# Final stage of a layer norm and mixture-of-experts kernel: the sum of shared and picked rows moves from VectorE to TensorE, and the normalising reads PSUM

## The chip, the core and the metric

The kernel runs on one core of a Trainium2 chip. The metric is the device time of one execution in microseconds (us), the median of several. Work is spread over TensorE (matmuls), VectorE, ScalarE, GpSimd and the DMA queues that SyncE and GpSimd issue to.

## The reference

The input x is 4 sequences of 1024 tokens with 128 features, 4096 tokens in all. Two sublayers follow each other, each closed by a layer norm without gain:

```python
x = layernorm(x + memory_mixer(x))            # cumulative sums of weighted cos/sin features, queries, silu, W_out
logits = x @ router_w.T                       # 8 experts, the best two are taken
out = sum_e mlp_e(x) * combine[:, e] + shared_mlp(x)   # mlp: square(relu(x @ w_fc.T)) @ w_proj.T, 512 wide
x = layernorm(x + out)                        # mean and variance over the 128 features, eps 1e-5
```

The last line is what this case is about. For one token it needs x plus the shared MLP (the "shared row"), the two expert results that the token was sent for (the "picked rows", each already multiplied by its weight), their sum, its mean and variance, and (sum - mean) / sqrt(variance + eps).

## The kernel before

Five functions make the program, and each hands every engine its piece in turn: memory (the mixer), dispatch (first layer norm, router, shared MLP, tokens written to a table by expert), routed (the expert MLPs) and finish. The first two take about 339 us of the span. routed goes over 46 tiles, 25 of 256 rows and then 21 of 128. For each tile SyncE loads rows of the table, TensorE transposes them (L1376), multiplies by the up weights into the tensors ph (L1388), ScalarE applies relu and square (L1434, L1443), TensorE multiplies by the down weights into po (L1401), VectorE scales by the router's weight (L1485) and GpSimd scatters the rows to pick_scratch in HBM, two places for each token. The four tensors ph, unused, po and px of routed take PSUM banks 0 to 6 (ph has two buffers of two banks), one bank is free.

dispatch leaves in y_all, in SBUF, x plus the shared MLP for all 4096 tokens: 32 columns of 128 tokens, 128 features each (L1193).

finish works in 8 groups of four columns, 512 tokens, 128 partitions by 512 numbers. Group g has a PSUM bank of its own, both[g].

- SyncE waits for the last scatters (L1527), then issues 16 loads (L1531), two for each group, 256 KB each, and after them 8 stores (L1537), each behind the ScalarE work of its group.
- TensorE (L1550) waits for the two loads of a group and adds the two picked rows by two matmuls with the identity into both[g]. Float32 matmuls stand in the trace as two passes each, so a group shows as four.
- VectorE adds the shared rows (add, L1578: both[g] + y_all into res, in SBUF), takes statistics (measure, L1586 bn_stats and L1590 bn_aggr, four of each), and in invert the reciprocal of the root (L1596) and the shift, -mean times it (L1598).
- ScalarE takes the square root of variance plus eps (L1561) and normalises, one instruction for each 128 by 128 column, scale and shift from SBUF (L1566).

The order on VectorE and ScalarE is written out by hand:

```python
            add(0)
            measure(0)
            for g in range(NG):
                if g + 1 < NG:
                    add(g + 1)
                invert(g)
                if g + 1 < NG:
                    measure(g + 1)
```

ScalarE takes the groups in turn, root and then four normalising instructions. Buffers res, stats, mv, xo and so on have S = 4 copies, so from group 4 on there are waits for the stores of earlier groups.

Of the kernel before, what the change touches and what calls it, by code (L numbers as in the profile page):

```python
# [14 lines left out]
P = 128  # L15
# [14 lines left out]
GT = 4  # L30
# [29 lines left out]
RoutedStage = namedtuple("RoutedStage", "sync scalar gpsimd tensor vector scattered")  # L60
# [1221 lines left out]
def routed(nc, outer, dis, ident, w1, w2, expert, start, table, pick_dram):  # L1282
# [4 lines left out]
    with ExitStack() as c:  # L1287
# [172 lines left out]
        def vector(dve):  # L1460
# [17 lines left out]
            def body(t, u):  # L1478
# [5 lines left out]
                for h in range(height(t)):  # L1484
# [6 lines left out]
                           scattered=[(scattered[t % U], passes(t)) for t in range(TILES - U, TILES)])  # L1491


def finish(nc, outer, rou, ident, y_all, eps, warm, pick_dram, out):

    with ExitStack() as c:
# [6 lines left out]
        S = 4  # L1503
        pick = sb("pick", [P, 2, NT, D])
        res = sb("res", [P, S, GT, D])
        stats = sb("stats", [P, S, GT, 6])
        mv = sb("mv", [P, S, GT, 2])
        std = sb("std", [P, S, GT])
        rstd = sb("rstd", [P, S, GT])
        shift = sb("shift", [P, S, GT])  # L1510
        xo = sb("xo", [P, S, GT, D])
# [3 lines left out]
        res_done = sem("res_done")  # L1515
# [5 lines left out]
        xo_done = sem("xo_done")  # L1521
        eps_set = sem("eps_set")
        stored = [sem(f"stored{i}") for i in range(S)]

        def sync(sp):
# [9 lines left out]
            def store(g):  # L1535
                sp.wait_ge(xo_done, g + 1)
                sp.dma_start(out[:, g * P:(g + 1) * P, :].rearrange("b p d -> p b d"), xo[:, g % S]  # L1537
                             ).then_inc(stored[g % S], 16)
# [4 lines left out]
            for i in range(S):  # L1543
                sp.wait_ge(stored[i], 16 * NG // S)

        def tensor(pe):
            for g in range(NG):
                pe.wait_ge(picked[g], 32)
                for r in range(2):
                    last = nc.tensor.matmul(both[g][:], ident[:],  # L1550
                                            pick[:, r, g * GT:(g + 1) * GT, :].rearrange("p t d -> p (t d)"),
                                            start=(r == 0), stop=(r == 1))
                last.then_inc(both_done, 1)

        def scalar(act):
            act.wait_ge(eps_set, 1)
            nc.scalar.activation(warm[:], eps[:], ACT.Sqrt)
            for g in range(NG):
                s = g % S
                act.wait_ge(var_done, g + 1)  # L1560
                nc.scalar.activation(std[:, s], mv[:, s, :, 1], ACT.Sqrt, bias=eps[:]).then_inc(std_done, 1)  # L1561
                act.wait_ge(shift_done, g + 1)
                if g >= S:
                    act.wait_ge(stored[s], 16 * (g // S))
                for t in range(GT):
                    last = nc.scalar.activation(xo[:, s, t, :], res[:, s, t, :], ACT.Identity,  # L1566
                                                bias=shift[:, s, t:t + 1], scale=rstd[:, s, t:t + 1])
                last.then_inc(xo_done, 1)

        def vector(dve):  # L1570
            nc.vector.memset(eps[:], EPS).then_inc(eps_set, 1)

            def add(g):
                s = g % S
                dve.wait_ge(both_done, g + 1)
                if g >= S:
                    dve.wait_ge(xo_done, g - S + 1)
                nc.vector.tensor_tensor(res[:, s].rearrange("p t d -> p (t d)"), both[g][:],  # L1578
                                        y_all[:, g * GT:(g + 1) * GT, :].rearrange("p t d -> p (t d)"), ALU.add
                                        ).then_inc(res_done, 1)  # L1580

            def measure(g):
                s = g % S
                dve.wait_ge(res_done, g + 1)
                for t in range(GT):
                    last = nc.vector.bn_stats(stats[:, s, t, :], res[:, s, t, :])  # L1586
                last.then_inc(stats_done, 1)
                dve.wait_ge(stats_done, g + 1)
                for t in range(GT):
                    last = nc.vector.bn_aggr(mv[:, s, t, :], stats[:, s, t, :])  # L1590
                last.then_inc(var_done, 1)

            def invert(g):
                s = g % S
                dve.wait_ge(std_done, g + 1)
                nc.vector.reciprocal(rstd[:, s], std[:, s]).then_inc(rstd_done, 1)  # L1596
# [68 lines left out]
```

## Time and profile before

| | |
|---|---|
| median of 3 runs | 514.8 us (514.63 to 515.39) |
| the profiled execution | 513.47 us, span 511.6 us, mean granted TensorE clock 0.967 |
| busy over the span | TensorE 88%, VectorE 73%, ScalarE 70%, GpSimd 58% |
| last matmul of routed starts | 476.98 us |
| first matmul of finish starts | 484.54 us |
| last matmul of finish ends | 500.42 us |
| last normalising instruction ends | 508.85 us |

Times are counted from the start of the span. The routed stage and everything before it are the same in both kernels; what differs is what happens behind 477 us, some 35 us of the span. The profiled execution was 1.3 us shorter than the median of the three runs.

### The profile page before, as it was taken

What the parts mean: (1) busy time and instruction counts of PE and PEld (TensorE: products, weight loads), DVE (VectorE), ACT (ScalarE), POOL (GpSimd) and SP (SyncE); (2) the same over time, 40 slices, a digit from 0 to 9 for tenths busy, and PEclk for the clock granted to TensorE, in tenths of its full rate; (3) what the DMA queues carried; (4) which work ended last, traced back from release to release, by engine and by line L of the source; (5) the groups of instructions that cost most, each with busy time, mean ns of one, the idle gap of its engine ahead of it and who ended that gap; (6) DMA issues with size and microseconds to landing.
All of it is one profiled execution on the core that took longest, in us unless ns stands there. A gap on an engine that the chain in (4) does not pass through costs nothing.

```text
span 511.6 us, 7508 instructions
## 1 busy us (share of the span) xinstructions
PE 450.6 (88%) x2162; PEld 293.2 (57%) x2162; DVE 374.9 (73%) x863; ACT 357.7 (70%) x545; POOL 294.5 (58%) x250
## 2 busy tenths in 40 slices
PE   8757899998999988887888999689999999999391
PEld 5313344433443333344666777479999999999340
DVE  6776999998999999999998976533433334555075
ACT  3839799998999999971555566427666666566256
POOL 3235567777677787873767677714455555655200
PEclk9979999999999999999799999979999999999897
DMA  8010010109955566000111111131222221221373
GB/s 264 4 43 0 1 43 1 44 2 375 350 210 209 211 222 229 32 1 2 45 42 49 36 49 57 54 90 52 68 69 78 65 64 57 70 57 54 102 279 113
DMA packets 39448, 48.55 MB, mean 95 GB/s; under 512 B 5408, under 2 KB 25058, under 8 KB 38896
## 3 DMA queue, kind: packets, MB, share of 16 engines
q1 hardware_dynamic: 34048, 39.06, 22.7%
q0 software_dynamic: 5216, 8.70, 5.5%
q8 instruction: 18, 0.29, 0.2%
q10 hardware_dynamic: 144, 0.31, 0.2%
q14 instruction: 22, 0.18, 0.1%
HBM read 19.17 MB, written 29.11 MB: 94 GB/s over the span
## 4 chain that ended last, share of the span: by engine, by line
DVE 41%; PE 35%; ACT 8%; issue 7%; POOL 4%; DMA 3%; DVEq 0%; ACTq 0%; POOLq 0%; SPq 0%
PE routed_ph L1388 13%; PE routed_po L1401 12%; DVE memory_y_raw L735 10%; DVE memory_prod L726 10%; DVE memory_feat L711 4%; PE dispatch_spo L927 3%; POOL table_scratch L1080 3%; ACT finish_xo L1566 2%; PE memory_nsum L585 2%; DVE dispatch_xrow L1148 2%; PE dispatch_sph L917 2%; PE routed_px L1376 1%; DVE memory_query L706 1%; DMA memory_feat<-memory_last_rows 1%; ACT memory_feat L377 1%
## 5 line engine op out<-in xcount | busy, mean ns | idle before, releaser
L465 POOL TENSOR_TENSOR memory_feat<-memory_feat,memory_p_tok 128x1024 f32<-128x1024 f32 x64 | 121.5, 1920 | 54.7 <-ACT memory_feat L377 54.7
L585 PE MATMUL memory_nsum<-memory_feat,tri 128*128 128x512 f32 x256 | 116.5, 598 | 10.8 <-ACT memory_last_rows L386 4.3
L1364 POOL DMA_INDIRECT pick_scratch<-routed_ob,routed_xg x71 | 70.9, 998 | 74.3 <-DVE routed_ob L1485 60.8
L585 PEld LDWEIGHTS memory_nsum<-memory_feat,tri 128*128 128x128 f32 x256 | 46.9, 190 | 70.0 <-issue 66.7
L1080 POOL DMA_INDIRECT table_scratch<-dispatch_xrow,dispatch_slot x64 | 61.8, 966 | 27.7 <-issue 17.1
L1434 ACT ACTIVATE routed_rel<-routed_ph 128x512 f32<-128x512 f32 x71 | 42.3, 597 | 46.1 <-PE routed_ph L1388 46.1
L1388 PE MATMUL routed_ph<-routed_xs,routed_w1c 128*128 128x256 f32 (+1 forms) x368 | 71.3, 337 | 0.9 <-DVE routed_w2c L1471 0.9
L1485 DVE TENSOR_SCALAR routed_ob<-routed_po,routed_xg 128x128 f32<-128x128 f32 x71 | 22.6, 348 | 67.2 <-PE routed_po L1401 67.2
L1401 PE MATMUL routed_po<-routed_w2c,routed_hid 128*128 128x128 f32 x568 | 71.1, 275 | 0.5 <-ACT routed_hid L1443 0.5
L726 DVE TENSOR_TENSOR memory_prod<-memory_nsum,memory_query 128x1024 f32<-128x1024 f32 x58 | 68.2, 1215 | 1.9 <-PE memory_nsum L585 1.9
L1401 PEld LDWEIGHTS routed_po<-routed_w2c,routed_hid 128*128 128x128 f32 x568 | 67.0, 192 | 0.8 <-ACT routed_hid L1443 0.7
L735 DVE TENSOR_REDUCE memory_y_raw<-memory_prod 128x128 f32<-128x2048 f32 x29 | 66.3, 2285 | 0.9
L386 ACT COPY memory_last_rows<-memory_nsum 32x1024 f32<-32x1024 f32 x56 | 54.9, 1005 | 8.4 <-DVE memory_prod L726 6.3
L1388 PEld LDWEIGHTS routed_ph<-routed_xs,routed_w1c 128*128 128x128 f32 x368 | 56.5, 191 | 5.6 <-ACT routed_xs L1425 1.1
L569 PE MATMUL memory_ph<-setup_th_f,setup_k_val 64*128 64x512 f32 x128 | 37.7, 666 | 12.0 <-DVE memory_feat L711 11.9
L711 DVE SCALAR_TENSOR_TENSOR memory_feat<-memory_feat,memory_ph 128x1024 f32<-128x1024 f32 x32 | 38.4, 1202 | 9.0 <-ACT memory_feat L368 9.0
L927 PEld LDWEIGHTS dispatch_spo<-w,dispatch_shid 128*128 128x128 f32 x256 | 34.6, 204 | 14.8 <-issue 13.0
L1443 ACT ACTIVATE routed_hid<-routed_rel 128x512 f32<-128x512 f32 x71 | 42.5, 638 | 0.0
L927 PE MATMUL dispatch_spo<-w,dispatch_shid 128*128 128x128 f32 x256 | 36.3, 290 | 5.7 <-DVE y_all L1193 5.7
L1013 ACT ACTIVATE dispatch_srel<-dispatch_sph 128x512 f32<-128x512 f32 x32 | 19.1, 597 | 31.6 <-PE dispatch_sph L917 31.6
L368 ACT ACTIVATE memory_feat<-memory_ph 128x1024 f32<-128x1024 f32 x32 | 32.7, 1023 | 9.4 <-PE memory_ph L569 8.7
L377 ACT ACTIVATE memory_feat<-memory_feat,memory_half_pi 128x1024 f32<-128x1024 f32 x32 | 36.4, 1139 | 0.0
(187 smaller groups left out, 662.1 us busy)
## 6 DMA issues: line engine op xcount, KB each, us to landing
table_scratch<-memory_blank SPq DMA_DIRECT2D x68, 260.0 KB, 2.8
finish_pick<-pick_scratch SPq DMA_DIRECT2D x16, 256.0 KB, 5.6
routed_xg<-table_scratch SPq DMA_DIRECT2D x25, 130.0 KB, 2.2
x_tok<-x SPq DMA_DIRECT2D x4, 512.0 KB, 3.9
w<-w_up SPq DMA_DIRECT2D x2, 1024.0 KB, 9.0
w<-w_down SPq DMA_DIRECT2D x2, 1024.0 KB, 11.1
out<-finish_xo SPq DMA_DIRECT2D x8, 256.0 KB, 2.3
routed_xg<-table_scratch SPq DMA_DIRECT2D x21, 65.0 KB, 1.9
```

What stands on the lines that cost most here:

```text
L386: nc.scalar.copy(last_rows[32 * b:32 * b + 32, h * NF:(h + 1) * NF], nsum[96:P, h * NF:(h + 1) * NF]).then_inc(rows_kept, 1)
L465: last = nc.gpsimd.tensor_tensor(v, v, pv, ALU.mult)
L585: last = nc.tensor.matmul(nsum[:, o:o + 512], tri[:], feat[:, i % U, h, q * 512:(q + 1) * 512], start=True, stop=True)
L711: nc.vector.scalar_tensor_tensor(v, v, -ROUND, ph[:], ALU.add, ALU.subtract).then_inc(frac_done, 1)
L726: nc.vector.tensor_tensor(products(i)[:, h, :].rearrange("p (q r c) -> p q r c", q=KQ, r=REP), nv, qv.unsqueeze(2).broadcast_to([P, KQ, RE ...
L735: nc.vector.tensor_reduce(y_raw[:, j % 2, b, :], products(i)[:, 0:2].rearrange("p h (c m) -> p c h m", m=M), AX.XY, ALU.add).then_inc(red_ ...
L927: last = nc.tensor.matmul(spo[:, t * D:(t + 1) * D], shid[:, g % 2, q, t * P:(t + 1) * P], w2[:, E, q, :], start=(q == 0), stop=(q == FC - 1))
L1080: nc.gpsimd.indirect_dma_start(out=table, in_=xrow[:, r, n, :], in_offset=None, out_offset=bass.IndirectOffsetOnAxis(ap=slot[:, r, n:n + 1 ...
L1364: nc.gpsimd.indirect_dma_start(out=pick_dram, in_=ob[:, u, h, :], in_offset=None, out_offset=bass.IndirectOffsetOnAxis(ap=xg[:, t % XU, h, ...
L1388: last = nc.tensor.matmul(ph[s][:, q * n:(q + 1) * n], w1c[:, u, q * P:(q + 1) * P], xs[:, s, 0:n], start=True, stop=True)
L1401: last = nc.tensor.matmul(po[:, h * D:(h + 1) * D], hid[:, s, q * n + h * P:q * n + (h + 1) * P], w2c[:, u, q, :], start=(q == 0), stop=(q ...
L1443: nc.scalar.activation(hid[:, s, o:o + FC * P], rel[:, n % 2, :], ACT.Square).then_inc(hid_done, 1)
```

## The change

- TensorE now makes the whole sum. Before the picked rows of any group, eight matmuls with the identity put the shared rows of y_all into the eight banks (start=True), in the order 4, 7, 6, 0 to 3, 5. Group 6's bank is px of routed, so it waits for the last copy out of it (x_kept); banks 0 to 3 are ph, so they wait for the last relu (rel_done); bank 5 is po, so it waits for the last scaling (kept). Then the picked rows are added to the same banks (start=False) group by group, in the order 0 to 7.
- VectorE's addition and the buffer res are gone. bn_stats reads both[g] in PSUM, and so does the normalising.
- Groups 3 and 7 are normalised on VectorE, by tensor_scalar with two scalars, (both - mean) * rstd. ScalarE keeps six groups, and its square roots are moved into the middle of the normalising of the group before.
- On VectorE measure(g + 1) now stands ahead of invert(g), from group 1 on.
- All small buffers and xo have 8 copies, so no wait on a store is left before the end, and the stores share one semaphore.

The diff of the functions, with the buffer declarations left out:

```diff
@@
+        BY_DVE = (3, 7)
...
@@ -1533,79 +1533,105 @@
                                  [:, g * GT:(g + 1) * GT, :]).then_inc(picked[g], 16)
 
             def store(g):
-                sp.wait_ge(xo_done, g + 1)
-                sp.dma_start(out[:, g * P:(g + 1) * P, :].rearrange("b p d -> p b d"), xo[:, g % S]
-                             ).then_inc(stored[g % S], 16)
+                if g in BY_DVE:
+                    sp.wait_ge(dve_done, BY_DVE.index(g) + 1)
+                else:
+                    sp.wait_ge(act_done, g + 1 - sum(d < g for d in BY_DVE))
+                sp.dma_start(out[:, g * P:(g + 1) * P, :].rearrange("b p d -> p b d"), xo[:, g]).then_inc(stored, 16)
             for g in range(NG):
                 load(g)
             for g in range(NG):
                 store(g)
-            for i in range(S):
-                sp.wait_ge(stored[i], 16 * NG // S)
+            sp.wait_ge(stored, 16 * NG)
 
         def tensor(pe):
-            for g in range(NG):
+            def shared(g):
+                nc.tensor.matmul(both[g][:], ident[:], y_all[:, g * GT:(g + 1) * GT, :].rearrange("p t d -> p (t d)"),
+                                 start=True, stop=False)
+
+            def picks(g):
                 pe.wait_ge(picked[g], 32)
                 for r in range(2):
                     last = nc.tensor.matmul(both[g][:], ident[:],
                                             pick[:, r, g * GT:(g + 1) * GT, :].rearrange("p t d -> p (t d)"),
-                                            start=(r == 0), stop=(r == 1))
+                                            start=False, stop=(r == 1))
                 last.then_inc(both_done, 1)
 
+            shared(4)
+            shared(7)
+            pe.wait_ge(rou.x_kept, TILES)
+            shared(6)
+            pe.wait_ge(rou.rel_done, rou.banks)
+            for g in range(4):
+                shared(g)
+            pe.wait_ge(rou.kept, TILES)
+            shared(5)
+            for g in range(NG):
+                picks(g)
+
         def scalar(act):
+            def root(g):
+                act.wait_ge(var_done, g + 1)
+                nc.scalar.activation(std[:, g], mv[:, g, :, 1], ACT.Sqrt, bias=eps[:]).then_inc(std_done, 1)
+
+            def normalise(g, half):
+                if half == 0:
+                    act.wait_ge(shift_done, g + 1)
+                for t in (2 * half, 2 * half + 1):
+                    last = nc.scalar.activation(xo[:, g, t, :], both[g][:, t * D:(t + 1) * D], ACT.Identity,
+                                                bias=shift[:, g, t:t + 1], scale=rstd[:, g, t:t + 1])
+                if half == 1:
+                    last.then_inc(act_done, 1)
+
             act.wait_ge(eps_set, 1)
             nc.scalar.activation(warm[:], eps[:], ACT.Sqrt)
-            for g in range(NG):
-                s = g % S
-                act.wait_ge(var_done, g + 1)
-                nc.scalar.activation(std[:, s], mv[:, s, :, 1], ACT.Sqrt, bias=eps[:]).then_inc(std_done, 1)
-                act.wait_ge(shift_done, g + 1)
-                if g >= S:
-                    act.wait_ge(stored[s], 16 * (g // S))
-                for t in range(GT):
-                    last = nc.scalar.activation(xo[:, s, t, :], res[:, s, t, :], ACT.Identity,
-                                                bias=shift[:, s, t:t + 1], scale=rstd[:, s, t:t + 1])
-                last.then_inc(xo_done, 1)
+            root(0)
+            normalise(0, 0)
+            normalise(0, 1)
+            root(1)
+            for g in (1, 2, 4, 5, 6):
+                if g == 4:
+                    root(4)
+                normalise(g, 0)
+                root(g + 1)
+                normalise(g, 1)
 
         def vector(dve):
             nc.vector.memset(eps[:], EPS).then_inc(eps_set, 1)
 
-            def add(g):
-                s = g % S
+            def measure(g):
                 dve.wait_ge(both_done, g + 1)
-                if g >= S:
-                    dve.wait_ge(xo_done, g - S + 1)
-                nc.vector.tensor_tensor(res[:, s].rearrange("p t d -> p (t d)"), both[g][:],
-                                        y_all[:, g * GT:(g + 1) * GT, :].rearrange("p t d -> p (t d)"), ALU.add
-                                        ).then_inc(res_done, 1)
-
-            def measure(g):
-                s = g % S
-                dve.wait_ge(res_done, g + 1)
                 for t in range(GT):
-                    last = nc.vector.bn_stats(stats[:, s, t, :], res[:, s, t, :])
+                    last = nc.vector.bn_stats(stats[:, g, t, :], both[g][:, t * D:(t + 1) * D])
                 last.then_inc(stats_done, 1)
                 dve.wait_ge(stats_done, g + 1)
                 for t in range(GT):
-                    last = nc.vector.bn_aggr(mv[:, s, t, :], stats[:, s, t, :])
+                    last = nc.vector.bn_aggr(mv[:, g, t, :], stats[:, g, t, :])
                 last.then_inc(var_done, 1)
 
             def invert(g):
-                s = g % S
                 dve.wait_ge(std_done, g + 1)
-                nc.vector.reciprocal(rstd[:, s], std[:, s]).then_inc(rstd_done, 1)
+                dve.wait_ge(var_done, g + 1)
+                nc.vector.reciprocal(rstd[:, g], std[:, g]).then_inc(rstd_done, 1)
                 dve.wait_ge(rstd_done, g + 1)
-                nc.vector.scalar_tensor_tensor(shift[:, s], mv[:, s, :, 0], -1.0, rstd[:, s], ALU.mult, ALU.mult
+                nc.vector.scalar_tensor_tensor(shift[:, g], mv[:, g, :, 0], -1.0, rstd[:, g], ALU.mult, ALU.mult
                                                ).then_inc(shift_done, 1)
 
-            add(0)
+            def normalise(g):
+                for t in range(GT):
+                    last = nc.vector.tensor_scalar(xo[:, g, t, :], both[g][:, t * D:(t + 1) * D], mv[:, g, t, 0:1],
+                                                   rstd[:, g, t:t + 1], ALU.subtract, ALU.mult)
+                last.then_inc(dve_done, 1)
+
             measure(0)
-            for g in range(NG):
-                if g + 1 < NG:
-                    add(g + 1)
-                invert(g)
+            invert(0)
+            measure(1)
+            for g in range(1, NG):
                 if g + 1 < NG:
                     measure(g + 1)
+                invert(g)
+                if g in BY_DVE:
+                    normalise(g)
 
         return FinishStage(sync=sync, scalar=scalar, tensor=tensor, vector=vector)
```

What stands in a row on TensorE at the end of the program, from the last routed tile on; both is the PSUM tensor of finish, pick the loaded rows:

```order
 L1388 MATMUL routed_ph<-routed_xs,routed_w1c 128x128 x4
 L1401 MATMUL routed_po<-routed_w2c,routed_hid 128x128 x8
-L1550 MATMUL finish_both<-finish_pick,ident 128x512 x16
+L1549 MATMUL finish_both<-y_all,ident 128x512 x8
+L1555 MATMUL finish_both<-finish_pick,ident 128x512 x16
 L65 UNCONDITIONAL_BRANCH
```

Eight matmuls of the shared rows now stand between the last down product and the sixteen of the picked rows.

VectorE at the start of finish, before (the number behind both is the group):

```order
L1571 MEMSET eps 128x1
L1578 TENSOR_TENSOR finish_res<-finish_both0,y_all 128x512
L1586 BN_STATS finish_stats<-finish_res 128x6 x4
L1590 BN_AGGR finish_mv<-finish_stats 128x2 x4
L1578 TENSOR_TENSOR finish_res<-finish_both1,y_all 128x512
L1596 RECIPROCAL finish_rstd<-finish_std 128x4
L1598 SCALAR_TENSOR_TENSOR finish_shift<-finish_mv,finish_rstd 128x4
```

VectorE in the middle of finish, in the changed kernel, around the first group that it normalises:

```order
L1605 BN_STATS finish_stats<-finish_both4 128x6 x4
L1609 BN_AGGR finish_mv<-finish_stats 128x2 x4
L1615 RECIPROCAL finish_rstd<-finish_std 128x4
L1617 SCALAR_TENSOR_TENSOR finish_shift<-finish_mv,finish_rstd 128x4
L1622 TENSOR_SCALAR finish_xo<-finish_both3,finish_mv,finish_rstd 128x128 x4
L1605 BN_STATS finish_stats<-finish_both5 128x6 x4
```

The addition is gone, statistics of group 4 stand ahead of the reciprocal of group 3, and the normalising of group 3 stands ahead of the statistics of group 5.

## Rows read from the trace of the kernel before

**Rows 1.** The chain that ended last, 476 to 494 us: start, us, what.
```profile
480.98 3.52 DMA finish_pick<-pick_scratch
484.54 3.80 PE finish_both L1550 x4
488.36 0.70 DVE finish_res L1578
489.08 0.88 DVE finish_stats L1586 x4
489.99 0.38 DVE finish_mv L1590 x4
...
491.26 1.65 ACT finish_xo L1566 x4
```

**Rows 2.** Timeline of ScalarE, end of the program: start, us, instruction, count [idle before].
```profile
504.92 1.65 ACT L1566 ACTIVATE finish_xo<-finish_res,finish_shift,finish_rstd 128x128 f32<-128x128 f32 x4 [0.44 <-DVE finish_shift L1598]
506.48 0.28 ACT L1561 ACTIVATE finish_std<-finish_mv,eps 128x4 f32<-128x4 f32 x1
507.20 1.65 ACT L1566 ACTIVATE finish_xo<-finish_res,finish_shift,finish_rstd 128x128 f32<-128x128 f32 x4 [0.44 <-DVE finish_shift L1598]
```

**Rows 3.** Windows: stretch, us, busy of the five engines, granted clock, DMA share, GB/s.
```profile
476.00:481.00 5.00, 1.13 (x8) 0.97 (x8) 0.36 (x2) 1.49 (x2) 1.96 (x2) 1.00 0.03 4
...
482.00:488.00 6.00, 3.46 (x4) 1.51 (x5) 0.00 (x0) 0.00 (x0) 0.00 (x0) 0.50 0.96 315
...
489.00:500.00 11.00, 11.00 (x27) 4.75 (x25) 10.13 (x55) 7.64 (x21) 0.00 (x0) 1.00 0.70 241
```

**Rows 4.** Timeline of all engines between the routed stage and finish.
```profile
476.12 1.13 PE L1401 MATMUL routed_po<-routed_w2c,routed_hid 128*128 128x128 f32 x8 [0.53 <-ACT routed_hid L1443]
...
477.29 0.35 DVE L1485 TENSOR_SCALAR routed_ob<-routed_po,routed_xg 128x128 f32<-128x128 f32 x1 [1.31 <-PE routed_po L1401]
```

**Rows 5.** Timeline of TensorE, matmul passes of the picked rows at full clock.
```profile
496.82 3.60 PE L1550 MATMUL finish_both<-finish_pick,ident 128*128 128x512 f32 x8
```

**Rows 6.** The load line L1531, one issue each: the second of group 1, and the last.
```profile
L1531 SPq DMA_DIRECT2D finish_pick<-pick_scratch x1: 431/431/431, 481.9 to 481.9; - x1
...
DMA to landing us min/median/max: 4.7/4.7/4.7
...
L1531 SPq DMA_DIRECT2D finish_pick<-pick_scratch x1: 433/433/433, 488.5 to 488.5; - x1
...
DMA to landing us min/median/max: 6.3/6.3/6.3
```

**Rows 7.** Timeline of VectorE, the last group.
```profile
504.81 0.86 DVE L1586 BATCH_NORM_STATS2 finish_stats<-finish_res 128x6 f32<-128x128 f32 x4
505.70 0.38 DVE L1590 BATCH_NORM_AGGREGATE finish_mv<-finish_stats 128x2 f32<-128x6 f32 x4
506.79 0.18 DVE L1596 RECIPROCAL finish_rstd<-finish_std 128x4 f32<-128x4 f32 x1 [0.71 <-ACT finish_std L1561]
507.00 0.16 DVE L1598 SCALAR_TENSOR_TENSOR finish_shift<-finish_mv,finish_rstd 128x4 f32<-128x4 f32 x1
```

**Rows 8.** Timeline of VectorE, pairs in a row that read PSUM.
```profile
303.20 0.68 DVE L1193 TENSOR_TENSOR y_all<-dispatch_spo,dispatch_xrow 128x512 f32<-128x512 f32 x1
303.80 0.68 DVE L1126 TENSOR_TENSOR dispatch_res<-dispatch_pb,x_tok 128x512 f32<-128x512 f32 x1
...
380.82 0.35 DVE L1485 TENSOR_SCALAR routed_ob<-routed_po,routed_xg 128x128 f32<-128x128 f32 x1 [2.20 <-PE routed_po L1401]
...
381.09 0.34 DVE L1485 TENSOR_SCALAR routed_ob<-routed_po,routed_xg 128x128 f32<-128x128 f32 x1
```

**Rows 9.** Groups by line and shape: busy us, mean ns, idle before them.
```profile
L1434 ACT ACTIVATE routed_rel<-routed_ph 128x512 f32<-128x512 f32 x71 | 42.3, 597 | 46.1 <-PE routed_ph L1388 46.1
...
L1443 ACT ACTIVATE routed_hid<-routed_rel 128x512 f32<-128x512 f32 x71 | 42.5, 638 | 0.0
```

**Rows 10.** DMA issues of the page: instruction, count, size, median us to landing.
```profile
out<-finish_xo SPq DMA_DIRECT2D x8, 256.0 KB, 2.3
```

More of the change, by code:

```diff
@@ L59 @@
 DispatchStage = namedtuple("DispatchStage", "sync scalar gpsimd tensor vector sent tabled experts_in")
-RoutedStage = namedtuple("RoutedStage", "sync scalar gpsimd tensor vector scattered")
+RoutedStage = namedtuple("RoutedStage", "sync scalar gpsimd tensor vector scattered x_kept rel_done banks kept")
 FinishStage = namedtuple("FinishStage", "sync scalar tensor vector")
@@ L1490, in routed @@
         return RoutedStage(sync=sync, scalar=scalar, gpsimd=gpsimd, tensor=tensor, vector=vector,
-                           scattered=[(scattered[t % U], passes(t)) for t in range(TILES - U, TILES)])
+                           scattered=[(scattered[t % U], passes(t)) for t in range(TILES - U, TILES)],
+                           x_kept=x_kept, rel_done=rel_done, banks=parts(TILES), kept=kept)
 def finish(nc, outer, rou, ident, y_all, eps, warm, pick_dram, out):
@@ L1501, in sem @@
             return outer.enter_context(nc.semaphore("finish_" + name))
-        S = 4
+        BY_DVE = (3, 7)
         pick = sb("pick", [P, 2, NT, D])
[L1505 to L1511, printed above, removed]
+        stats = sb("stats", [P, NG, GT, 6])
+        mv = sb("mv", [P, NG, GT, 2])
+        std = sb("std", [P, NG, GT])
+        rstd = sb("rstd", [P, NG, GT])
+        shift = sb("shift", [P, NG, GT])
+        xo = sb("xo", [P, NG, GT, D])
         both = [c.enter_context(nc.psum_tensor(f"finish_both{g}", [P, GT * D], F32)) for g in range(NG)]
@@ L1514, in finish @@
         both_done = sem("both_done")
-        res_done = sem("res_done")
         stats_done = sem("stats_done")
@@ L1520, in finish @@
         shift_done = sem("shift_done")
-        xo_done = sem("xo_done")
+        act_done = sem("act_done")
+        dve_done = sem("dve_done")
         eps_set = sem("eps_set")
-        stored = [sem(f"stored{i}") for i in range(S)]
+        stored = sem("stored")
         def sync(sp):
```

## The prediction

> **What bounds the kernel now.** Nothing ahead of the last routed matmul changes, so I read only what lies behind it. The chain of waits comes first [rows 1]. It goes from the landing of group 0's second load at 484.5 us through four matmul passes of 3.80 us, the addition (0.70), the statistics (0.88) and their aggregation (0.38), and by root, reciprocal and shift to the first normalising at 491.26. From there one group costs 2.28 us: the normalising of the last two groups starts at 504.92 and 507.20 [rows 2], and (507.20 - 491.26) / 7 is 2.28 as well. The reader should see what these 2.28 us are made of: four normalising instructions occupy ScalarE for 1.56 us (504.92 to 506.48), then comes the root of the next group (0.28) and, on VectorE, reciprocal and shift (506.79 to 507.16), for which ScalarE stands idle 0.44. So the additions of groups 1 to 7 are beside the path, and ScalarE with its round trip to VectorE is the bound.
>
> The windows show the second thing [rows 3]: with TensorE idle, its granted clock is at the upper level (2.4 GHz, 1.00) until 481 and at the lower (1.2 GHz, 0.50) from 482 to 488. Group 0's matmuls run at the lower one, and it is back up from 489. At the upper level eight passes take 3.60 us, the last of them lasting 0.59 [rows 5]: 0.43 us from one to the next, 1.72 for a group. The 3.80 of group 0 would be 3 x 0.43 + 0.59 = 1.88.
>
> **The shared rows on TensorE.** Eight matmuls, two passes each, make 16 x 0.43 = 6.9 us. The last down product starts its eighth pass at 476.98 and the engine is free at about 477.1 [rows 4]. The banks are free in time: px and ph were last read before that last down product started, and po is released by the scaling that ends at 477.64, before the eighth matmul (group 5) has its turn. So the shared rows end being issued at 484.0, against 484.5 for the first landing. They cost nothing, and the cover is the wait for scatters and loads, with 0.5 us to spare; any lateness beyond that goes fully into the path. Since TensorE then never idles for more than half a microsecond, the clock should stay up. Statistics of group 0 start at 484.54 + 1.88 + 0.04 = 486.46 instead of 489.08: 1.92 from the clock, 0.70 from the addition.
>
> **When the groups are ready.** Group 1's second load is issued at 481.9 and lands 4.7 later, at 486.6 [rows 6]; TensorE would be ready for it at 486.3, so it is ready at 488.5. After that TensorE is the slower of the two: 490.25, 491.96, 493.7, ... 498.8 for groups 2, 3, 4, ... 7, while the last load lands at 488.5 + 6.3 = 494.8 [rows 6] and is wanted at 496.9. The first stores now start while loads still run. One store of 256 KB takes the place of one load, about 0.7 us at the 16 loads' pace ((494.8 - 484.5) / 14), and group 7 has 2.1 us to spare, so I cost it at nothing.
>
> **VectorE.** Per group: statistics 0.91 to the start of the aggregation, which lets the next instruction in 0.30 later, then reciprocal and shift 0.29 together [rows 7], in all 1.50. Statistics of group 0 start at 486.46, of 1 at 488.54, then with the banks: group 4's at 493.67. Behind them comes invert(3), and at 495.17 VectorE is ready for the normalising of group 3. The price of one normalising instruction from PSUM has no row. One that reads PSUM with one scalar starts 0.27 after another (381.09 - 380.82) and lasts 0.34 [rows 8]. With a second scalar I take 0.33 from one to the next and 0.41 for the last, bounds 0.27 and 0.41. So statistics 5 start at 495.17 + 1.32 = 496.49, statistics 6 at 497.99, 7 at 499.49.
>
> bn_stats from PSUM has no row either. From SBUF four take 0.86 with 0.28 for one, 0.19 to 0.20 apart [rows 7]. Additions that read PSUM start 0.60 apart for 512 columns [rows 8]; with 128 columns that is 0.15 plus a fixed part which these rows don't show to be larger than that of bn_stats from SBUF. I take 0.20, with 0.27 (the PSUM pair of rows 8) as the upper bound and no lower price than 0.20.
>
> The Trainium skill, "VectorE: DVE Perf Modes", section "The TRN2 errata", speaks against the change here: it gives VectorE a fixed part of 120 cycles with a PSUM source against 58 with an SBUF source, at 0.96 GHz. As an estimate from that page each bn_stats would be 65 ns dearer, and by it the end would be about 0.9 us later than my sum.
>
> **ScalarE, the tail.** Its normalising instructions are 0.39 apart (1.56 / 4) [rows 2]. Read from PSUM, a 512-column activation takes 597 ns against 638 from SBUF [rows 9], so I take 0.35, a half group 0.70; bounds 0.35 and 0.39. A root takes 0.19 of the engine. When shift(4) is done at 498.07, these stand on ScalarE ahead of root(7): both halves of group 4, both of 5, the first of 6, and the roots of 5 and 6: 5 x 0.70 + 2 x 0.19 = 3.88, from 498.11 to 501.99. Root(7) ends at 502.27, reciprocal and shift at 502.59, and VectorE's four instructions (3 x 0.33 + 0.41) at 504.0. Group 6 ends on ScalarE at 503.0.
>
> **Sum.** Last result at 504.0 against 508.85. Behind it stood 2.75 us (issue, 2.3 to land [rows 10], end). Group 6's store is issued 1.0 us ahead of group 7's, about the time its data moves, so I add 0.05. The gain is 4.8 us. The profiled execution took 513.47 for a span of 511.6 and should come to **508.7**, with a span of 506.8. It was 1.3 below the median of the runs; against that median of 514.8 I forecast **510.0**. With the low prices (0.27 for VectorE's normalising) the end is at 503.5, with all high ones (0.27 for statistics, 0.39 on ScalarE, 0.41 for the normalising) at 505.7: 509.4 to 511.7.
>
> **Rivals.**
> 1. *PSUM is dear for VectorE's statistics.* Each of the 32 costs 0.27 instead of 0.20, 0.28 for a group. The statistics of groups 4 and 5, and the wait ahead of root(6), each push the ScalarE tail by about that, so the end is at 505.1, time 511.1. For it: TENSOR_SCALAR from PSUM at 0.27 apart [rows 8]; against: it carries a scalar operand that bn_stats has not.
> 2. *The loads set the pace.* The early stores and uneven landings hold every group from 1 on back by 1 us: end at 505.0, time 511.0. For it: group 1 waits for its load already [rows 6]; against: two spare microseconds at group 7.
> 3. *Slower than before: the shared rows come late.* If TensorE ran them at the lower clock level, one pass taking 0.86, they would take 13.7 us, end at 490.8 instead of 484.0, and the whole stage would follow: 504.0 + 6.3 - 0.4 (group 1's wait is gone) = 509.9, that is 1.1 later than before: 515.9. It decides from the point where picked rows start later than 489.8; between there and 484.5 it only eats the gain, and near 489 gives no change. Against: clock 1.00 at 476 to 481 even without matmuls [rows 3]. A bank released late would do the same, but the last release is at 477.64 [rows 4].
> 4. *No change*, because the shared rows don't hide and start picked rows at 488.8 to 490.8.
>
> **How the numbers follow.** Forecast 0.60, rival 1 0.22, rival 2 0.08, rival 3 0.05, rival 4 0.05. About 1.0 us (0.2%) is what a measurement of this kernel can tell from no change. The first three are faster by more: 0.90; the same 0.05; slower 0.05. The range takes in the forecast's own bounds, rivals 1 and 2, and the spread of the runs (0.2 below their median, 0.6 above): 508.7 to 512.0.
>
> **What would show it.** In the changed profile: 16 passes of shared rows from about 477.1 to 484.0, granted clock 1.00 from 476 to 500; first statistics at 486.5; bn_stats rows 0.20 apart; statistics of groups 1 to 4 at 1.7 us from one to the next, set by TensorE, and from 5 on by VectorE; ScalarE without a gap from 498.1 to 502.3; last xo at 504.0 on VectorE. I would be wrong if the clock falls inside the shared rows, if the statistics are 0.26 apart, or if TensorE waits for loads behind group 1.

## Result and profile after

The changed kernel takes 509.44 us (median of 6 runs, 508.54 to 510.66) against 514.71 (6 runs, 513.16 to 515.39): ratio 0.9905, 95% interval 0.9882 to 0.9927, so 3.8 to 6.1 us faster. The forecast was 510.0, and 508.7 for the profiled execution, which took 509.45 with a span of 507.6. On another chip the same two kernels stood 510.35 to 513.8, ratio 0.9926 (0.9910 to 0.9942). A kernel has a second, slower state in some of its runs, and every ratio here is taken over the other runs alone.

The last down product of routed starts at 477.34 in this trace and at 476.12 before; no line ahead of it was changed, and over all traces on quiet chips this point lies anywhere from 475.2 to 477.8. That scatter is as large as the effects looked at here. So every trace below is also read from its own last down product on. Before, the last result is 32.73 us behind it and the span ends at 35.48; in the changed kernel 27.52 and 30.26. By this measure the gain is 5.2 us, where 4.8 was forecast.

TensorE, timeline (start, us, instruction, count [idle before]), first the picked rows before, then the changed kernel:

```profile
484.54 15.89 PE L1550 MATMUL finish_both<-finish_pick,ident 128*128 128x512 f32 x32 [7.28 <-DMA finish_pick<-pick_scratch]
...
477.34 1.13 PE L1401 MATMUL routed_po<-routed_w2c,routed_hid 128*128 128x128 f32 x8 [0.54 <-ACT routed_hid L1443]
478.31 7.03 PE L1549 MATMUL finish_both<-y_all,ident 128*128 128x512 f32 x16
485.59 14.19 PE L1555 MATMUL finish_both<-finish_pick,ident 128*128 128x512 f32 x32 [0.25 <-DMA finish_pick<-pick_scratch]
```

The 7.28 us of idling that stood ahead of the picked rows are 0.25 now: the shared rows fill them. The 32 passes took 15.89 before and take 14.19. The windows (stretch, us, busy of PE, PEld, DVE, ACT, POOL, granted clock, DMA share, GB/s) show why; against [rows 3] the clock stays at its upper level:

```profile
476.00:481.00 5.00, 4.46 (x23) 2.87 (x22) 0.71 (x3) 2.66 (x4) 2.95 (x3) 1.00 0.02 4
481.00:483.00 2.00, 2.00 (x6) 0.84 (x5) 0.00 (x0) 0.00 (x0) 0.00 (x0) 1.00 0.10 15
483.00:485.00 2.00, 2.00 (x6) 0.76 (x4) 0.00 (x0) 0.00 (x0) 0.00 (x0) 1.00 0.82 270
485.00:500.00 15.00, 14.54 (x33) 5.89 (x32) 10.93 (x69) 6.54 (x21) 0.00 (x0) 1.00 0.91 312
```

VectorE, timeline, the first, second, third, fifth and sixth statistics and the end:

```profile
487.61 0.89 DVE L1605 BATCH_NORM_STATS2 finish_stats<-finish_both 128x6 f32<-128x128 f32 x4 [8.74 <-PE finish_both L1555]
...
489.58 0.88 DVE L1605 BATCH_NORM_STATS2 finish_stats<-finish_both 128x6 f32<-128x128 f32 x4
...
491.24 0.89 DVE L1605 BATCH_NORM_STATS2 finish_stats<-finish_both 128x6 f32<-128x128 f32 x4 [0.37 <-PE finish_both L1555]
...
494.67 0.89 DVE L1605 BATCH_NORM_STATS2 finish_stats<-finish_both 128x6 f32<-128x128 f32 x4 [0.15 <-PE finish_both L1555]
...
496.15 1.36 DVE L1622 TENSOR_SCALAR finish_xo<-finish_both,finish_mv,finish_rstd 128x128 f32<-128x128 f32 x4
497.43 0.88 DVE L1605 BATCH_NORM_STATS2 finish_stats<-finish_both 128x6 f32<-128x128 f32 x4
...
503.21 0.18 DVE L1615 RECIPROCAL finish_rstd<-finish_std 128x4 f32<-128x4 f32 x1 [1.21 <-ACT finish_std L1575]
...
503.50 1.36 DVE L1622 TENSOR_SCALAR finish_xo<-finish_both,finish_mv,finish_rstd 128x128 f32<-128x128 f32 x4
```

The handover that was forecast is plain here. Statistics of groups 2 to 4 wait for TensorE and start 1.72 apart (those of group 1 stand behind the reciprocal and shift of group 0). Those from group 5 on wait for nothing, since VectorE is late by its own normalising of group 3: it holds the engine for 1.28 (496.15 to 497.43), and group 5, due 1.72 behind group 4 at 496.39, starts 1.04 late. ScalarE, timeline, the stretch with group 4 and the last root:

```profile
499.02 0.81 ACT L1581 ACTIVATE finish_xo<-finish_both,finish_shift,finish_rstd 128x128 f32<-128x128 f32 x2 [2.59 <-DVE finish_shift L1617]
...
502.83 0.34 ACT L1575 ACTIVATE finish_std<-finish_mv,eps 128x4 f32<-128x4 f32 x1
```

ScalarE idles 2.59 us in the middle of the stage, and then it is busy and late: root(7) starts at 502.83 though its variance is there at 501.67 (501.29 + 0.38 of aggregation), and VectorE waits 1.21 for it.

### The profile page after: what moved, and what is told of

Its sections match the earlier page's. It is cut to its first block, busy times and chain, and to the rows that moved or that the text cites. A ratio compares the mean times of both kernels' runs of the same rounds, so it can differ in the third digit from the quotient of the medians.

```text
span 507.6 us, 7530 instructions
## 1 busy us (share of the span) xinstructions
PE 457.0 (90%) x2178; PEld 295.1 (58%) x2178; DVE 372.6 (73%) x863; ACT 353.5 (70%) x537; POOL 294.8 (58%) x250
## 4 chain that ended last, share of the span: by engine, by line
DVE 43%; PE 36%; issue 7%; ACT 6%; POOL 4%; DMA 3%; DVEq 0%; POOLq 0%; ACTq 0%; SPq 0%
PE routed_ph L1388 13%; PE routed_po L1401 12%; DVE memory_y_raw L735 11%; DVE memory_prod L726 10%; DVE memory_feat L711 4%; PE dispatch_spo L927 3%; POOL table_scratch L1080 3%; DVE dispatch_xrow L1148 2%; PE finish_both L1555 2%; PE memory_nsum L585 2%; PE dispatch_sph L917 2%; PE routed_px L1376 1%; DVE memory_query L706 1%; DMA memory_feat<-memory_last_rows 1%; ACT memory_feat L368 1%
## 5 line engine op out<-in xcount | busy, mean ns | idle before, releaser
L585 PE MATMUL memory_nsum<-memory_feat,tri 128*128 128x512 f32 x256 | 118.1, 605 | 10.2 <-ACT memory_last_rows L386 3.9
```

Of the source, the lines that this page charges most:

```text
L585: last = nc.tensor.matmul(nsum[:, o:o + 512], tri[:], feat[:, i % U, h, q * 512:(q + 1) * 512], start=True, stop=True)
```

## The experiments

All times in this table are from the start of the last down product, in the profiled execution. "Behind" is the last result less the end of the last matmul.

| kernel | picked rows start | last matmul ends | last result | behind | span ends |
|---|---|---|---|---|---|
| before | 8.42 | 24.31 | 32.73 | 8.42 | 35.48 |
| changed | 8.25 | 22.44 | 27.52 | 5.08 | 30.26 |
| changed, again | 8.20 | 23.54 | 28.61 | 5.07 | 31.31 |
| before, TensorE kept busy | 8.41 | 22.82 | 30.99 | 8.17 | 33.78 |
| shared rows late | 9.01 | 32.11 | 36.43 | 4.32 | 39.21 |
| shared rows twice | 14.70 | 28.60 | 33.67 | 5.07 | 36.44 |
| all groups on ScalarE | 8.25 | 23.50 | 28.22 | 4.72 | 30.97 |
| the same, old order | 8.31 | 22.80 | 28.82 | 6.02 | 31.51 |
| only group 7 on VectorE | 8.29 | 23.36 | 27.68 | 4.32 | 30.37 |
| and root(7) first | 8.20 | 22.82 | 26.30 | 3.48 | 29.67 |
| and the filler | 7.55 | 22.43 | 25.92 | 3.49 | 29.24 |

The runs but those of the quiet chips (the first pair, "changed, again", "old order", "only group 7" and the first "root(7) first") fell on two chips on which the kernel before itself took 541 to 556 us. I call them unsettled; ratios from there have intervals 1% to 6% wide. Their traces are used for the stretch behind the last down product only. There the instruction durations are those of the quiet chips, and the granted clock is 1.00 up to the last matmul in all of them but "shared rows late".

**Before, with TensorE kept busy.** The shared rows go into the banks and are overwritten by the picked rows; VectorE still adds them.

```diff
@@ before, tensor(pe)
+            def shared(g):
+                nc.tensor.matmul(both[g][:], ident[:], y_all[:, g * GT:(g + 1) * GT, :].rearrange("p t d -> p (t d)"),
+                                 start=True, stop=True)
+
+            shared(4)
+            shared(7)
...
             for g in range(NG):
                 pe.wait_ge(picked[g], 32)
```

> Kernel before, with the eight matmuls of the shared rows put ahead of the picked rows as in the change, but closed on their own and then overwritten by the picked rows, so that they only keep TensorE busy; the sum is still VectorE's. Times from the start of the last down product to the end of the span, which was 35.5 us before and 30.3 in the changed kernel. Theory (the clock is 1.9 of the gain, and the rest is the chain behind it): granted clock 1.00 throughout, group 0 ready 1.9 us earlier, then 2.28 us for a group as before, 33.5 us in all, time about 1.9 below before. Rival (the clock gains nothing because ScalarE's chain is fed by something else, or the loads bound the groups): 35.0 or more.

Windows of this kernel, columns as above:

```profile
507.00:515.00 8.00, 7.82 (x24) 3.64 (x23) 0.36 (x2) 1.19 (x2) 1.96 (x2) 1.00 0.31 91
515.00:520.00 5.00, 4.77 (x10) 1.84 (x11) 2.65 (x12) 0.30 (x1) 0.00 (x0) 1.00 1.01 360
```

The clock stays up. First statistics are 11.16 us behind the last down product instead of 12.96, the last result 1.74 earlier, the span 1.70 shorter. The clock part of the theory stands (1.9 expected, 1.7 to 1.8 measured), got by work that computes nothing of use. The ratios, 0.991 (0.981 to 1.001) and, run again, 1.005 (0.993 to 1.018), decide nothing.

> The kernel before with TensorE only kept busy, once more, for its time: its profile showed 33.8 us from the last down product against 35.5 before; about 1.7 us faster than before, ratio 0.997.

The second trace showed 34.39, so 1.09 below before and not the 1.7 expected. The last result is 0.66 later than in the first trace: 0.26 because the picked rows start later, and 0.40 because group 1 waits for its load. TensorE there, and ScalarE's first normalising in the first and in the second trace:

```profile
527.44 12.28 PE L1564 MATMUL finish_both<-finish_pick,ident 128*128 128x512 f32 x28 [0.37 <-DMA finish_pick<-pick_scratch]
```

```profile
520.19 1.65 ACT L1580 ACTIVATE finish_xo<-finish_res,finish_shift,finish_rstd 128x128 f32<-128x128 f32 x4 [0.59 <-DVE finish_shift L1612]
```

```profile
530.47 1.65 ACT L1580 ACTIVATE finish_xo<-finish_res,finish_shift,finish_rstd 128x128 f32<-128x128 f32 x4 [1.02 <-DVE finish_shift L1612]
```

In the order of before, invert(0) stands behind add(1) on VectorE, so a late group 1 holds back even the first normalising.

**Shared rows late.**

```diff
@@ changed kernel, tensor(pe)
-            shared(4)
...
-            shared(5)
             for g in range(NG):
+                pe.wait_ge(picked[g], 32)
+                shared(g)
                 picks(g)
```

> Changed kernel with each group's shared rows directly ahead of its picked rows, behind the wait for its loads; nothing else is moved. Theory (the shared rows are free only because they lie in the wait for the loads): TensorE idles and falls to the lower clock level, then needs six passes of 0.43 us for a group, 2.58, more than the loads (1.35) and more than VectorE (1.50) ask for; TensorE sets the pace to the end, 38.3 us from the last down product, about 3 us slower than before. Rival (TensorE has slack in this stage and the gain is VectorE's missing addition): at most 33 us.

Windows (columns as above), then TensorE's timeline, the first group and two late ones:

```profile
520.00:524.00 4.00, 0.10 (x1) 0.13 (x1) 0.00 (x0) 0.00 (x0) 0.00 (x0) 0.50 0.81 262
524.00:529.00 5.00, 5.00 (x7) 2.18 (x8) 0.00 (x0) 0.00 (x0) 0.00 (x0) 0.55 0.96 326
529.00:547.00 18.00, 18.00 (x42) 7.61 (x41) 11.54 (x72) 8.40 (x26) 0.00 (x0) 1.00 0.46 154
```

```profile
523.90 2.05 PE L1549 MATMUL finish_both<-y_all,ident 128*128 128x512 f32 x2 [7.89 <-DMA finish_pick<-pick_scratch]
525.74 3.24 PE L1555 MATMUL finish_both<-finish_pick,ident 128*128 128x512 f32 x4
...
539.12 1.02 PE L1549 MATMUL finish_both<-y_all,ident 128*128 128x512 f32 x2
539.98 1.88 PE L1555 MATMUL finish_both<-finish_pick,ident 128*128 128x512 f32 x4
541.69 1.02 PE L1549 MATMUL finish_both<-y_all,ident 128*128 128x512 f32 x2
```

The clock is down for the first group and up again from the second on. A group takes TensorE 2.57 us (541.69 - 539.12) to the end, and the span ends 3.7 us later than before: 39.2 where 38.3 was expected, 0.8 of the difference because the loads landed later (9.01 against 8.25). Behind the wait, the sum on TensorE is a loss, by the fallen clock and by two more passes in each group; in the wait it is free. The ratio, 1.0052 (0.9962 to 1.0141), leans that way and isn't clear of 1.

**Shared rows twice.**

```diff
@@ changed kernel, tensor(pe)
             shared(5)
+            for g in range(NG):
+                shared(g)
             for g in range(NG):
                 picks(g)
```

> Changed kernel with the shared rows made twice (the first set is overwritten), which doubles the work in the cover: picked rows start about 6.6 us later than in the changed kernel, at the upper clock level. Theory (cover exhausted after some 0.25 us, all lateness goes into the path): 36.8 us from the last down product, 1.3 slower than before, the slower rival of the prediction made real. Rival (part of the lateness is absorbed, because from group 5 on VectorE and ScalarE and not TensorE set the end): 34 us or less.

```profile
501.32 13.90 PE L1549 MATMUL finish_both<-y_all,ident 128*128 128x512 f32 x32
515.06 13.90 PE L1555 MATMUL finish_both<-finish_pick,ident 128*128 128x512 f32 x32
```

The timeline of TensorE has no gap: 6.45 us of lateness at the start of the picked rows came out as 6.15 at the last result and 6.18 at the end of the span (36.44 and, run again, 36.47). That is 1.0 more than before in the trace, which is the size of the slower rival (1.1). The ratios, 0.987 (0.976 to 0.998) and, run again, 0.999 (0.993 to 1.006), don't bear it out: the first says the opposite, from two runs, and both carry the scatter of the part ahead. So the mechanism is shown by the traces, that the program is slower by it is not.

> The changed kernel with the shared rows made twice, once more, for its time: its profile showed 36.4 us from the last down product against 35.5 before; about 1 us slower than before, ratio 1.002.

**All groups on ScalarE.**

```diff
-        BY_DVE = (3, 7)
+        BY_DVE = ()
@@ scalar(act)
-            for g in (1, 2, 4, 5, 6):
+            for g in range(1, NG):
```

> Changed kernel with no group normalised on VectorE; ScalarE takes all eight, in the same interleaved order. Theory (from the rows of the changed kernel: VectorE's normalising of group 3 holds the statistics of group 5 back by 1.3 us while ScalarE idles 2.6 us, so it gives back what ScalarE saves): 29.9 us from the last down product, no slower than the changed kernel's 30.3. Rival (two groups off ScalarE are the part that gives the gain beyond clock and addition): 8 x 1.56 + 8 x 0.28 + waits on ScalarE, 2.1 us later than the changed kernel, 32.4.

TensorE and then ScalarE of this kernel, timelines:

```profile
524.98 1.98 PE L1555 MATMUL finish_both<-finish_pick,ident 128*128 128x512 f32 x4 [0.25 <-DMA finish_pick<-pick_scratch]
527.94 12.29 PE L1555 MATMUL finish_both<-finish_pick,ident 128*128 128x512 f32 x28 [0.98 <-DMA finish_pick<-pick_scratch]
```

```profile
539.13 0.29 ACT L1575 ACTIVATE finish_std<-finish_mv,eps 128x4 f32<-128x4 f32 x1
539.32 1.64 ACT L1581 ACTIVATE finish_xo<-finish_both,finish_shift,finish_rstd 128x128 f32<-128x128 f32 x4
540.84 0.29 ACT L1575 ACTIVATE finish_std<-finish_mv,eps 128x4 f32<-128x4 f32 x1
541.03 1.64 ACT L1581 ACTIVATE finish_xo<-finish_both,finish_shift,finish_rstd 128x128 f32<-128x128 f32 x4
```

The last result is 4.72 behind the last matmul, where the changed kernel has 5.08 (and 5.07 in its second trace, where TensorE waited as long as here): giving two groups to VectorE made it 0.36 worse. ScalarE takes a group in 1.71 (540.84 - 539.13), just TensorE's pace, with no idle time in these lines. The span is 30.97 and not 29.9, because here TensorE waited 0.98 for group 1's second load, of which the next run tells more. The ratio, 0.984 (0.972 to 0.996), is from the unsettled chip.

**The changed kernel again.**

> The changed kernel once more, on the chip of the next three: 30.3 us from the last down product to the end of the span, about 5.2 below before.

```profile
485.99 1.99 PE L1555 MATMUL finish_both<-finish_pick,ident 128*128 128x512 f32 x4 [0.20 <-DMA finish_pick<-pick_scratch]
489.05 12.28 PE L1555 MATMUL finish_both<-finish_pick,ident 128*128 128x512 f32 x28 [1.08 <-DMA finish_pick<-pick_scratch]
```

31.31 instead of 30.26, with 5.07 behind the last matmul as against 5.08: the difference is the 1.08 us in which TensorE waits between group 0 and group 1. The second load of group 1 (issued 1.3 us behind the first of the 16) took 5.4 us to land here, 4.1 in the first trace of the changed kernel and 4.7 before [rows 6]:

```profile
L1531 SPq DMA_DIRECT2D finish_pick<-pick_scratch x1: 432/432/432, 483.6 to 483.6; - x1
...
DMA to landing us min/median/max: 5.4/5.4/5.4
```

Before, TensorE reached group 1 only 3.6 us after group 0, at the lower clock and 1.4 us behind the landing, so a microsecond of scatter was covered. It is not ScalarE's pace that covered it: in "kept busy" ScalarE sets the pace too, and there the wait went into the end. Now it goes into the end whole. It may be part of why the gain was 5.3 us on one chip and 3.5 on the other; that is not shown.

**Old order.**

```diff
@@ all groups on ScalarE, vector(dve)
             measure(0)
-            invert(0)
-            measure(1)
-            for g in range(1, NG):
-                if g + 1 < NG:
-                    measure(g + 1)
-                invert(g)
+            for g in range(NG):
+                invert(g)
+                if g + 1 < NG:
+                    measure(g + 1)
@@ scalar(act)
+            for g in range(NG):
+                root(g)
+                normalise(g, 0)
+                normalise(g, 1)
```

> Changed kernel with all groups on ScalarE and the order of before on both engines (invert(g) ahead of measure(g+1); root, then four normalising instructions). Theory: the round trip to VectorE is back in every group, 1.41 for four normalising instructions from PSUM plus root, reciprocal and shift 0.72, so 2.13 a group; 31.5 us from the last down product, 4.0 below before, 1.2 above the changed kernel: that is what the new order is worth. Rival (order is worth nothing once the addition is gone): 30.3 or less.

```profile
500.00 0.30 ACT L1575 ACTIVATE finish_std<-finish_mv,eps 128x4 f32<-128x4 f32 x1
500.75 1.50 ACT L1581 ACTIVATE finish_xo<-finish_both,finish_shift,finish_rstd 128x128 f32<-128x128 f32 x4 [0.44 <-DVE finish_shift L1611]
502.13 0.30 ACT L1575 ACTIVATE finish_std<-finish_mv,eps 128x4 f32<-128x4 f32 x1
```

ScalarE's timeline has the 0.44 of waiting for the shift back, and a group takes 2.13 (502.13 - 500.00), as computed; 31.51 expected as 31.5. In time it is 511.03, ratio 0.9945 (0.9930 to 0.9959), beside 510.35 for the changed kernel on the same chip. TensorE hardly waits for group 1 in this trace, so it doesn't show what a late one would cost in this order.

**Only group 7 on VectorE.**

```diff
-        BY_DVE = (3, 7)
+        BY_DVE = (7,)
@@ scalar(act)
-            for g in (1, 2, 4, 5, 6):
-                if g == 4:
-                    root(4)
+            for g in range(1, 7):
```

> Changed kernel with group 3 given back to ScalarE and only group 7 normalised by VectorE. Theory: statistics of groups 5 to 7 start when TensorE has them ready (1.7 apart) and ScalarE has no long gap; 29.5 us from the last down product, 0.8 below the changed kernel. Rival (ScalarE becomes the bound with seven groups): 30.9, ScalarE 1.5 later less what it idled.

VectorE, timeline, the last two groups:

```profile
499.53 0.89 DVE L1603 BATCH_NORM_STATS2 finish_stats<-finish_both 128x6 f32<-128x128 f32 x4 [0.15 <-PE finish_both L1555]
500.46 0.38 DVE L1607 BATCH_NORM_AGGREGATE finish_mv<-finish_stats 128x2 f32<-128x6 f32 x4
...
502.15 0.18 DVE L1613 RECIPROCAL finish_rstd<-finish_std 128x4 f32<-128x4 f32 x1 [1.06 <-ACT finish_std L1575]
```

Statistics of group 7 now wait for TensorE, 0.04 behind its last matmul, and the last result is 4.32 behind it, 0.76 less than in the changed kernel. The span is 30.37 with 0.81 of waiting for group 1. 508.45 us, ratio 0.9886 (0.9868 to 0.9904): this interval and that of the changed kernel on the same chip (0.9910 to 0.9942) don't touch. The medians are 1.9 us apart, though, and the edit moves 0.76 in the traces; the rest stays open. VectorE's wait of 1.06 for root(7) is what is left to take.

**And root(7) first.**

```diff
-            for g in range(1, 7):
+            for g in range(1, 6):
                 normalise(g, 0)
                 root(g + 1)
                 normalise(g, 1)
+            root(7)
+            normalise(6, 0)
+            normalise(6, 1)
```

> As the run with only group 7 on VectorE, and root(7) moved ahead of the normalising of group 6 on ScalarE, so that VectorE's last group doesn't wait for it. Theory: root(7) starts when its variance is there; 28.7 us from the last down product, 1.6 below the changed kernel, time about 507.9. Rival (group 6 on ScalarE then ends last): 29.5, no gain over the run before.

TensorE, timeline of the picked rows:

```profile
483.43 3.76 PE L1555 MATMUL finish_both<-finish_pick,ident 128*128 128x512 f32 x8 [0.20 <-DMA finish_pick<-pick_scratch]
487.48 10.57 PE L1555 MATMUL finish_both<-finish_pick,ident 128*128 128x512 f32 x24 [0.29 <-DMA finish_pick<-pick_scratch]
```

3.48 behind the last matmul, 1.6 below the changed kernel as expected, but the span is 29.67 and not 28.7. 0.38 of that is the last matmul, at 22.82 instead of 22.44: here it is group 2 that waits for its load, behind the eight passes of groups 0 and 1. The rest lies behind the last result: 3.37 to the end of the span, where it was 2.74. Groups 6 and 7 are done 0.3 us apart and their stores issued 0.4 apart, and group 7's takes 2.8 us to land where it took 2.3 in the changed kernel. A store moves data for about a microsecond (DMA share in tenths over 501 to 504.9 us, and GB/s):

```profile
DMA  9999940000006999999989989898997200000000
GB/s 305 284 289 294 273 111 5 0 0 0 0 0 184 299 299 236 221 305 341 326 263 294 289 268 315 268 299 278 299 289 237 69 0 0 0 0 0 0 0 0
```

The two stores run as one block of 2 us. In time this kernel has 508.24, ratio 0.9902 (0.9885 to 0.9919), not to be told from the one before it. Once more, on the unsettled chip, the trace gave 3.48 behind the last matmul and 29.95, ratio 0.990 (0.973 to 1.006), with 0.40 of waiting for group 1.

> The kernel with only group 7 on VectorE and root(7) first, once more beside the filler kernel: last result 3.5 us behind the last matmul; 28.9 to 30 us from the last down product, by how late group 1's second load lands.

**And the filler.**

```diff
@@ tensor(pe), picks(g)
-                pe.wait_ge(picked[g], 32)
                 for r in range(2):
+                    pe.wait_ge(picked[g][r], 16)
@@
+            picks(0)
             pe.wait_ge(rou.kept, TILES)
             shared(5)
-            for g in range(NG):
+            for g in range(1, NG):
                 picks(g)
```

> As the run with root(7) first, with two edits on TensorE: each load has a semaphore of its own, so that a group's first picked row is added before the second load lands, and group 5's shared rows move behind group 0's picked rows, where they fill the wait for group 1's second load. In the runs so far that wait was 0 to 1.2 us (the second load of group 1 landed 5.4 to 6.7 us after the first issue, and 13.9 us of matmuls took 14.2 to 15.3), and it went whole into the end. Theory: first statistics 0.8 earlier; last matmul at 22.4 us from the last down product in every run instead of 22.4 to 23.5; 3.5 us behind it the last result; 28.6 to 28.8 us to the end of the span, time about 507. Rival (TensorE has no waits worth filling): as the run with root(7) first, 29.0 to 29.7.

```profile
523.71 1.98 PE L1555 MATMUL finish_both<-finish_pick,ident 128*128 128x512 f32 x4 [0.41 <-DMA finish_pick<-pick_scratch]
525.53 1.02 PE L1549 MATMUL finish_both<-y_all,ident 128*128 128x512 f32 x2
526.38 12.21 PE L1555 MATMUL finish_both<-finish_pick,ident 128*128 128x512 f32 x28
```

The picked rows start at 7.55, and the shared rows of group 5 cover the wait for group 1: these lines show no idling of TensorE after its first wait, and the last matmul at 22.43 where 22.4 was expected. The span, 29.24, is the shortest of all; the 28.6 to 28.8 expected left out the overlapping stores, 0.6 here as well. Its ratio, 0.989 (0.958 to 1.020), tells nothing, so that it is faster in time stays open.

## Why the prediction was right

- *What bounded the kernel.* Right, ScalarE with its round trip: with the old order and all groups on ScalarE the round trip is there again, 2.13 a group.
- *The clock.* Right. The shared rows alone, without any change to the sum, moved first statistics by 1.80 and the last result by 1.74; the forecast said 1.92. The first pass of the picked rows has 0.1 more than steady pace, which the 1.88 for group 0 left out (485.59 to 487.61 is 2.02, not 1.92).
- *The shared rows are free.* Right. Counted as in the forecast, from pass to pass, 0.4 us was to spare (0.97 + 16 x 0.43 = 7.85 against 8.25) instead of 0.5, since the loads landed 0.17 sooner; the timeline shows 0.25 of idling, because it counts the last pass to its end.
- *When the groups are ready.* This is the step that failed in kind, though it cost little: group 1's wait was put at a fixed 0.3 us. The changed kernel's first trace shows none. The load came in time, and it is luck that the sum held: the 32 passes took 14.19 against 13.90 in "shared rows twice", where nothing waits, and these 0.29, spread over the first three groups, took the place of the 0.3. In the other traces with this order on TensorE the idle time ahead of group 1 was 0.37 and 0.40 in two, 0.81, 0.98 and 1.08 in three, and none to speak of in two; in one more, group 2 waited 0.29, which the prediction had named as a sign that it would be wrong. Rival 2 had the right price for this (1 us) and one half of the cause, uneven landings. The other half, early stores, was not it: the waits come before any store is issued, and the last load landed 18.7 us behind the last down product in the changed kernel and 18.8 before, though two stores had been issued by then. With three waits of 0.8 us or more, its chance of 0.08 was too low.
- *VectorE.* Right to within 0.2 us. Counted from the first picked pass, statistics 5, 6 and 7 were due at 11.95, 13.45 and 14.95 and came at 11.84, 13.31 and 14.78. The normalising from PSUM was put at 0.33 apart and 0.41 for the last; four took 1.36 with a mean of 0.402, which is 0.32 apart. bn_stats was put at its SBUF price, and rival 1 falls with it: four from PSUM take 0.88 to 0.89 against 0.86 to 0.87. The rule in "VectorE: DVE Perf Modes" of the Trainium skill, section "The TRN2 errata", would by an estimate from its cycle counts have made the four 0.26 dearer; the measurement decides, and it says 0.02.
- *ScalarE, the tail.* Right: from the first half of group 4 to root(7) 3.88 was forecast and 3.81 measured (499.02 to 502.83); four instructions take 1.50, so 0.35 apart. The 0.19 of a root had no row in the forecast; the changed trace has 0.18 (499.72 to 499.90).
- *The sum.* Last result 19.46 behind the first picked pass, 19.27 measured; 0.17 more from the earlier landing; together the 5.2. The low bound has a slip of 0.1: an end at 503.5 makes 509.5, not 509.4.

Where the 5.2 us come from, by the runs, at the last result:

- 1.74, the clock (from before to "kept busy").
- 2.17, the addition and the reads from PSUM (from there to "old order"). Of this 0.83 lies ahead of the first statistics: the addition, and 0.1 of an earlier landing. 1.05 is seven groups at 2.13 instead of 2.28, and the rest is in the first and the last normalising.
- 1.66, the order of measure and invert and the root in mid-group (from there to "all on ScalarE", counted with the last matmul at 22.44 as in the changed kernel: 22.44 + 4.72 = 27.16).
- -0.36, the two groups on VectorE. This step was not costed apart in the forecast. Group 7 on VectorE is good, 4.32 behind the last matmul against 4.72 with none: it needs no shift and ends the chain. Group 3 holds the statistics of group 5 by 1.0 us while ScalarE, relieved of it, idles.

## What to carry to other kernels

An idle stretch of TensorE ahead of a DMA-bound stage can take work that another engine does later on the path; here it paid twice, since it also kept the clock up, and it must fit the gap: work past the gap's end came out nearly whole. When a stage is made faster, look for what the old pace had covered: a load that scattered by a microsecond without being seen became the largest source of scatter in the stretch behind the last down product. Work moved to another engine for balance should be placed where that engine waits; here it cost more than it gave where it stood ahead of the statistics that feed the other engine.

## What was not expected of the hardware

- Between identical loads the landing time scatters: the fourth of the 16 took 4.1 to 5.4 us from issue over these traces of quiet chips.
- bn_stats of 128 by 128 costs the same from PSUM and from SBUF to within 5 ns each (mean 283 against 278).
- The stores of groups 6 and 7, 256 KB each and issued 0.4 us apart, left 3.37 us behind the last result; issued 1.0 apart they left 2.74.
- At the upper clock four passes take 1.98 to 1.99 us when TensorE has just waited, and 1.88 when it has not.
